# A two-layer transformer block on one core: opening work of ScalarE, VectorE, GpSimd and TensorE put in another order

## Chip, cores and metric

The kernel runs on 1 core of one Trainium2 chip. The metric is device microseconds (us) of one launch; lower is better. Engines are named as in the profile: PE (TensorE), DVE (VectorE), ACT (ScalarE), POOL (GpSimd), SP (the queue that issues DMAs). Each engine works through its own queue in order; semaphores tie the queues together.

## What is computed

Two adaLN layers are applied to x of shape 2 x 2048 x 128 (batch, tokens, features).

```python
mod = (silu(c) @ wmod)                      # six rows of 128 per batch: sa, ca, ga, sb, cb, gb
ga, gb = sign(ga) * max(|ga|, 0.25), sign(gb) * max(|gb|, 0.25)
h = layernorm(x) * (1 + ca) + sa
x = x + ga * attention(h)
h = layernorm(x) * (1 + cb) + sb
x = x + gb * ffn(h)
```

Layer 0's attention has q, k and v projections, rotary tables on q and k, and a mask that lets each token see itself, all before it and one after. Its feed-forward quantises inputs and weights in blocks of 16 to FP4 (scale = largest magnitude / 6, values rounded to the FP4 grid), and computes silu(gate) * up, then down. Layer 1's attention scores are h qk h^T, causal, and its feed-forward is a mixture of 8 experts with 2 chosen per token plus one shared expert.

## The kernel before

The work of a batch is written as 32 slots: slot s is one tile of 128 query tokens, slots 0 to 15 of layer 0's attention and 16 to 31 of layer 1's. Four tiles make a group of 512 tokens. Each engine has a loop over the slots, written out by hand, and other work (projections of the next group, layer norms, the feed-forward six and eight slots behind) is placed in it by slot numbers. In slot s PE computes the scores of tile s + 1 (`score_products`, L859 and L867), transposes the probabilities of tile s (L985) and multiplies them with the values (L1007); DVE takes the maximum of the new scores (`maximum`, L1836) and finishes the tile (`finish`, L1858 and L1859); ACT computes the exponentials (L1399) and copies the transposes (L1425).

**The opening** comes ahead of the slots. PE runs `WARM_UP` matmuls on ones (L818), transposes the conditioning vectors (L821), and, once the first modulation matrix has landed, multiplies it with silu(c) to get columns of scales (`columns`, L812). DVE turns them into gains, normalises the first group (`first_normalise`, L1600), PE transposes it (L788), ACT scales it (L1272), and PE projects keys and queries (`project_0`, L799). DVE rotates them (`open_rotate`, L1622 to L1626), ACT writes the rounded halves (`first_round`, L1299: fp32r high part), DVE the low parts (`open_low`, L1632). PE meanwhile computes layer 1's columns, the first values (L879), and `FIRST_WAIT` matmuls whose results nobody reads (`keep_clock`, L794); then come the first scores.

**Groups 1 to 3 of layer 0.** For each, DVE normalises (`normalise(2, ...)`, L1799, four tiles), PE transposes (L788), ACT scales (L1352), PE projects keys (in slots 0, 2, 4) and queries (slots 1, 3, 5) with L799, DVE multiplies with the tables (`rotate`, L1819), POOL sums (`rope_sum`, L710), ACT rounds (`round_rope`, L1453), and POOL takes the low part (`rope_low`, L716). POOL also computes 1/sqrt of the variance (`first_rsqrt`, L635) ahead of each normalisation and, from slot 4 on, the modulation of the feed-forward's input (`modulate_1`, L675 and L677).

**FP4 weights.** DVE scales them (L1649 to L1658) and builds the step of the grid (`fp4_grid`, L1663 and L1664, at the end of slot 0); POOL rounds them in three passes for each of gate, up and down (`round_fp4_weights`, L660, L662, L664; slots 1, 2 and 3, after `first_rsqrt`); PE transposes them (L804) and ACT copies them (`turned_fp4_weights`, L1306 to L1310), with a scaling of the down weights by the gains in slot 4 (L1497). In slot 4 DVE also prepares layer 1's gains (`layer1_gains`, L1573 to L1577 and L1673), ahead of its rotation of group 3's keys, and after the slot quantises the feed-forward's first input (`fp4_input`, from L1876 on).

```python
FP4_W_ROUND_SLOTS, FP4_W_TURN_SLOTS, FP4_W_GATE_SLOT = {1: 0, 2: 1, 3: 2}, {3: 2, 4: 3, 5: 4, 6: 5}, 4
WARM_UP, FIRST_WAIT = 12, 18
```

Of the kernel before, what the change touches and what calls it, by code (L numbers as in the profile page):

```python
# [24 lines left out]
BANK = 512  # L25
# [15 lines left out]
ACT = mybir.ActivationFunctionType  # L41
# [5 lines left out]
def score_chunks(layer, i):  # L47


    w = (i + 1) * P  # L50
    chunks = [(c, min(BANK, w - c)) for c in range(0, w, BANK)]
    if layer == 0 and i < TILES - 1:
        chunks[-1] = (chunks[-1][0], chunks[-1][1] + 1)
    return chunks
# [51 lines left out]
def early_group(slot, first):  # L106

    g, off = divmod(slot - first, 2)
    return g if off == 0 and 1 <= g < GROUPS else None
# [90 lines left out]

FP4_W_ROUND_SLOTS, FP4_W_TURN_SLOTS, FP4_W_GATE_SLOT = {1: 0, 2: 1, 3: 2}, {3: 2, 4: 3, 5: 4, 6: 5}, 4
FP4_W_BANKS, GAINS_SLOT = {2: 2, 3: 2, 4: 3, 5: 3}, 4
WARM_UP, FIRST_WAIT = 12, 18
NORM0_SLOT = K0_SLOT - 2
NORM1_SLOT, NORM2_SLOT, NORM3_SLOT = GROUP - 1, DOWN_LAG + GROUP - 1, TILES + GROUP - 1
FP4_SLOT = GROUP
# [51 lines left out]
def build(nc, x, cos, sin, wq, wk, wv, w_gate, w_up, w_down, c0, wmod0, qk, ov, gate_w, lb_bias,  # L260
          e_gate, e_up, e_down, s_gate, s_up, s_down, c1, wmod1, out):
    ctx = ExitStack()
    with ctx:
# [56 lines left out]
        tick = sb("tick", [P, 1])  # L320
# [81 lines left out]
        def bank(n, a=0, b=BANK, rows=P):  # L402
            return ps[0:rows, n * BANK + a:n * BANK + b]
# [3 lines left out]
        TURN, OUT_AT, GATE, UP = 4, 5, 6, 7  # L407
# [32 lines left out]
        first_high = sem("first_high")  # L440
# [10 lines left out]
        roped = sem("roped")  # L451
# [150 lines left out]
        def _(pool):  # L602
# [50 lines left out]
            def round_fp4_weights(k):  # L653

                name = "gud"[k]
                cols = slice(fp4_at[name], fp4_at[name] + (INNER if name == "d" else K_TILES * P))
                step = slice(cols.start // BLOCK, cols.stop // BLOCK)
                part = fp4_q[:, cols]
                pool.wait_ge(fp4_scaled, 1)
                pool.tensor_tensor(part, part, fp4_abs[:, cols], ALU.add).then_inc(fp4_rounded, 1)  # L660
                pool.wait_ge(fp4_rounded, 3 * k + 1)
                pool.tensor_tensor(part, part, fp4_abs[:, cols], ALU.subtract).then_inc(fp4_rounded, 1)  # L662
                pool.wait_ge(fp4_rounded, 3 * k + 2)
                pool.tensor_tensor(blocks(part), blocks(part), fp4_s[:, 1, step].unsqueeze(2).to_broadcast(  # L664
                    [P, step.stop - step.start, BLOCK]), ALU.mult).then_inc(fp4_rounded, 1)

            for b in range(BATCH):
# [64 lines left out]
                def rope_lows(s):  # L732
                    if early_group(s, K0_SLOT + 1) is not None:
                        rope_low(early_group(s, K0_SLOT + 1), 0)
                    if early_group(s, Q0_SLOT + 1) is not None:
                        rope_low(early_group(s, Q0_SLOT + 1), 1)
# [8 lines left out]
                for s in range(SLOTS):  # L745
                    at = lambda first: group_at(s, first)
                    if s < FP4_SLOT:
                        rope_lows(s)
                    if early_group(s, K0_SLOT) is not None:
                        rope_sum(early_group(s, K0_SLOT), 0)  # L750
                    if early_group(s, Q0_SLOT) is not None:
                        rope_sum(early_group(s, Q0_SLOT), 1)
                    if at(NORM1_SLOT + 1) is not None:
                        modulate_1(at(NORM1_SLOT + 1))
                    if at(Q1_SLOT) is not None:
                        q1_low(at(Q1_SLOT))
                    if ffn_tile(s, FFN_LAG) is not None:
                        hq_scaled(s - FFN_LAG)
                    if s >= FP4_SLOT:
                        rope_lows(s)  # L760
                    if b + 1 == BATCH and s == MOE_W_LOW_SLOT:
                        for k in range(-(-SPLIT_AT_ONCE // BANK)):
                            moe_w_low(k)
                    if early_group(s, NORM0_SLOT) is not None:
                        first_rsqrt(b * GROUPS + early_group(s, NORM0_SLOT) + 1)
                    if b == 0 and s in FP4_W_ROUND_SLOTS:
                        round_fp4_weights(FP4_W_ROUND_SLOTS[s])
                    if b + 1 < BATCH and s in (NEXT_SLOT - 2, NEXT_SLOT):
                        first_rsqrt((b + 1) * GROUPS + (s == NEXT_SLOT) + 1)
                    if s % GROUP == GROUP - 1:  # L770
                        scale_and_shift(1 + (at(NORM2_SLOT) is not None), b * 2 * GROUPS + s // GROUP + 1)
                    if at(NORM2_SLOT + 2) is not None:
                        keys_low(at(NORM2_SLOT + 2))
                    if at(FP4_SLOT) is not None:
                        xq_scaled(at(FP4_SLOT))
                    if b + 1 == BATCH:
                        if s == UNSEL_CLEAR_SLOT:
                            pool.wait_ge(v_proj_ready, BATCH * 2 * GROUPS)
                            pool.wait_ge(keys_ready, BATCH * GROUPS)
                            pool.memset(hT[:], 0.0).then_inc(unsel_zeroed, 1)  # L780
# [462 lines left out]

        @block.scalar
        def _(act):
            act.wait_ge(c_turned, 1)
            act.activation(silu_c[:], bank(TURN, 0, 2 * BATCH), ACT.Silu).then_inc(silu_ready, 1)
            act.wait_ge(zeroed, 10)
# [31 lines left out]
            rows = ps[:, 0:BATCH * BANK].rearrange("p (b n) -> p b n", b=BATCH)  # L1280
            act.activation(mod_row[:, :, 0, :], rows[:, :, 0:P], ACT.Copy)
            act.activation(mod_row[:, :, 1, :], rows[:, :, P:2 * P], ACT.Identity, bias=one).then_inc(rows_copied, 1)
            act.wait_ge(weights_turned, 2)
            act.activation(wv_g[:].rearrange("p b n -> p (b n)"), src[:, 0:BATCH * P], ACT.Copy).then_inc(weights_ready, 1)
            act.wait_ge(columns_ready, 3)
# [5 lines left out]
            ins.then_inc(mods_ready, 1)  # L1291
            act.wait_ge(rows_ready, 2)
            act.activation(ga1_row[:].rearrange("p b n -> p (b n)"), src[:, 0:BATCH * P], ACT.Copy).then_inc(rows_copied, 1)
            act.activation(tick[:], one, ACT.Exp)

            def first_round(which, src):

                act.wait_ge(roped, 2 * which + 2)
                act.activation((k_parts, q_parts)[which][0][:, 0:BANK], bank(src), ACT.Copy).then_inc(first_high, 1)  # L1299

            def turned_fp4_weights(n):

                act.wait_ge(weights_turned, n + 1)
# [21 lines left out]
                act.activation(probs[:, 0, start:start + width], ps[:, start:start + width], ACT.Exp,  # L1325
                               bias=neg_max[:, 0:1]).then_inc(exp_done, 1)

            first_round(0, UP)
            put_v_at(0, 0, GATE)
            first_round(1, 3)  # L1330
            first_exp(-1)
            for b in range(BATCH):
                def filled(key):
# [225 lines left out]
        def _(dve):  # L1559
# [227 lines left out]
            for b in range(BATCH):  # L1787
# [168 lines left out]

                for s in range(SLOTS):
                    following = len(score_chunks(*divmod(s + 1, TILES))) if s + 1 < SLOTS else 0
                    if following:
                        maximum(s + 1, 0)  # L1960
                    if b and s == 0:
# [29 lines left out]
                    if b + 1 == BATCH:  # L1991
                        route_in(s)
                    finish(s)
                    if b == 0 and s == 0:
                        fp4_grid()
                    if group_at(s, FP4_SLOT) is not None:
                        fp4_input(group_at(s, FP4_SLOT))
                    if group_at(s, LOGIT_SLOT) is not None:
# [98 lines left out]
```

## Time and profile before

| | us |
|---|---|
| runs, median of 3 | 669.61 (666.71 to 670.39) |
| profiled execution | 664.82 |
| its span in the trace | 663.0 |
| PE busy | 607.0 (92%) |
| DVE busy | 467.8 (71%) |
| ACT busy | 355.3 (54%) |
| POOL busy | 247.2 (37%) |

The span runs from the first to the last recorded instruction; 1.82 us of the profiled execution lie around it. Of the chain of work that ended last, 67% of the span is on PE, 15% on DVE, 9% on ACT, 4% on POOL. A busy PE is not one at its peak.

### The profile page before, as it was taken

The numbers are of one execution on the slowest core, as the hardware profiler recorded it, in microseconds if no ns is written. First come the engines' busy times: TensorE is split into PE (matmuls) and PEld (weight loads), VectorE is DVE, ScalarE is ACT, GpSimd is POOL, SyncE is SP. The second block draws the span as 40 slices with busy tenths as digits, with TensorE's granted clock in tenths as the row PEclk, the third lists the DMA queues.
The fourth block names the chain that finished last, engine by engine and source line by source line (L and its number), as shares of the span: only waits on it lengthen the run. The fifth ranks groups of instructions, "written<-read, shape, count | busy, mean of one in ns | idle before, by whom it ended". The sixth has DMA issues, their size and how long they took to land.

```text
span 663.0 us, 11002 instructions
## 1 busy us (share of the span) xinstructions
PE 607.0 (92%) x3758; PEld 478.1 (72%) x3780; DVE 467.8 (71%) x1265; ACT 355.3 (54%) x740; POOL 247.2 (37%) x305
## 2 busy tenths in 40 slices
PE   7977899988878899999989998978999999999997
PEld 5645677876666777886768787766677888777775
DVE  4867689786797456826658978679756674787765
ACT  3424454565545464554346456565566556666554
POOL 4256565454674322004465636457452100000000
PEclk9989999999999999999989999999999999999999
DMA  8300000000000000000000000020000000000111
GB/s 258 97 0 2 1 1 1 1 0 1 1 0 1 1 1 1 1 1 0 1 1 1 1 1 1 0 61 2 0 2 1 1 1 1 1 1 16 33 33 48
DMA packets 12494, 9.65 MB, mean 15 GB/s; under 512 B 1868, under 2 KB 10904, under 8 KB 12440
## 3 DMA queue, kind: packets, MB, share of 16 engines
q1 hardware_dynamic: 12440, 8.95, 4.5%
q8 instruction: 31, 0.51, 0.3%
q14 instruction: 23, 0.19, 0.1%
HBM read 6.84 MB, written 2.10 MB: 13 GB/s over the span
## 4 chain that ended last, share of the span: by engine, by line
PE 67%; DVE 15%; ACT 9%; POOL 4%; issue 4%; DVEq 0%; ACTq 0%; POOLq 0%
PE ps L1007 14%; PE ps L859 11%; PE ps L985 8%; PE ps L1191 5%; PE ps L799 4%; PE ps L1193 4%; PE ps L1192 4%; ACT xn L1359 2%; PE ps L1033 2%; PE ps L1034 2%; PE ps L1051 2%; PE ps L794 2%; POOL rstd L644 1%; PE ps L879 1%; DVE row_max L1836 1%
## 5 line engine op out<-in xcount | busy, mean ns | idle before, releaser
L1425 ACT ACTIVATE probsT<-ps 128x512 f32<-128x512 f32 (+3 forms) x160 | 85.4, 534 | 159.0 <-PE ps L985 159.0
L1007 PE MATMUL ps<-v_sb,probsT 128*128 128x129 f32 (+1 forms) x1124 | 152.0, 278 | 2.6 <-ACT probsT L1427 2.6
L1007 PEld LDWEIGHTS ps<-v_sb,probsT 128*128 128x128 f32 (+1 forms) x1124 | 137.8, 191 | 7.3 <-ACT probsT L1427 4.0
L1836 DVE TENSOR_REDUCE row_max<-ps 128x1 f32<-128x512 f32 (+2 forms) x144 | 87.4, 619 | 53.2 <-PE ps L867 26.7
L985 PE MATMUL ps<-ident,probs 128*128 128x128 f32 (+1 forms) x562 | 90.6, 277 | 16.1 <-ACT hT L1352 7.8
L985 PEld LDWEIGHTS ps<-ident,probs 128*128 128x128 f32 (+1 forms) x562 | 63.6, 139 | 48.0 <-issue 43.6
L1399 ACT ACTIVATE probs<-ps,neg_max 128x512 f32<-128x512 f32 (+7 forms) x158 | 93.1, 621 | 7.7 <-DVE neg_max L1843 7.0
L683 POOL TENSOR_TENSOR hq<-ha,hp 128x352 f32<-128x352 f32 x32 | 29.9, 935 | 100.9 <-DVE hp L1886 100.9
L859 PE MATMUL ps<-k_high,q_high 128*128 128x512 f32 (+5 forms) x100 | 42.5, 425 | 6.9 <-ACT probs L1399 6.9
L643 POOL TENSOR_SCALAR minus_mean<-mv 128x4 f32<-128x4 f32 (+1 forms) x16 | 3.8, 237 | 105.1 <-DVE veps L1586 104.9
L1858 DVE RECIPROCAL rsum<-ps 128x1 f32<-128x1 f32 x64 | 10.5, 164 | 41.6 <-PE ps L1007 41.2
L859 PE MATMUL ps<-h_high,q_high 128*128 128x512 f32 (+2 forms) x80 | 35.9, 449 | 3.1 <-POOL q_low L729 3.1
L1520 ACT ACTIVATE probs<-ps 128x512 f32<-128x512 f32 x40 | 24.0, 600 | 26.4 <-PE ps L1184 18.5
L859 PE MATMUL ps<-k_high,q_low 128*128 128x512 f32 (+5 forms) x100 | 34.6, 346 | 0.0
L859 PE MATMUL ps<-k_low,q_high 128*128 128x512 f32 (+5 forms) x100 | 34.5, 345 | 0.0
L1900 DVE SCALAR_TENSOR_TENSOR silu_g<-silu_g,ps 128x352 f32<-128x352 f32 x32 | 16.5, 515 | 23.7 <-ACT silu_g L1407 23.7
L1051 PE MATMUL ps<-w_dg,hqT 128*128 128x128 f32 (+1 forms) x192 | 28.0, 282 | 4.5 <-ACT hqT L1412 4.5
L685 POOL TENSOR_TENSOR hq<-hq,hp 128x352 f32<-128x352 f32 x32 | 29.9, 936 | 2.5
L1359 ACT ACTIVATE xn<-x_sb,shift,rstd 128x128 f32<-128x128 f32 x64 | 26.1, 482 | 8.3 <-POOL shift L646 8.3
L1793 DVE BATCH_NORM_STATS2 bn<-x_sb 128x6 f32<-128x128 f32 x112 | 28.4, 287 | 2.2
L1051 PEld LDWEIGHTS ps<-w_dg,hqT 128*128 128x128 f32 (+1 forms) x192 | 24.6, 191 | 7.0 <-ACT hqT L1412 6.3
L859 PE MATMUL ps<-h_high,q_low 128*128 128x512 f32 (+2 forms) x80 | 29.3, 366 | 0.0
(294 smaller groups left out, 1399.1 us busy)
## 6 DMA issues: line engine op xcount, KB each, us to landing
out<-x_sb SPq DMA_DIRECT2D x7, 256.0 KB, 2.3
hT_all<-in_L_wmod SPq DMA_DIRECT2D x2, 384.0 KB, 4.5
x_sb<-in_L_attn_x SPq DMA_DIRECT2D x2, 256.0 KB, 3.8
rope_cos<-table_cos SPq DMA_DIRECT2D x2, 256.0 KB, 4.5
rope_sin<-table_sin SPq DMA_DIRECT2D x2, 256.0 KB, 5.6
x_sb<-in_L_attn_x SPq DMA_DIRECT2D x1, 512.0 KB, 6.1
rope_cos<-table_cos SPq DMA_DIRECT2D x1, 512.0 KB, 7.1
rope_sin<-table_sin SPq DMA_DIRECT2D x1, 512.0 KB, 7.3
```

Source lines behind the costliest of these rows:

```text
L683: pool.tensor_tensor(hq[:, n % 2, :], ha[:], hp[:], ALU.add).then_inc(hq_step, 1)
L685: pool.tensor_tensor(hq[:, n % 2, :], hq[:, n % 2, :], hp[:], ALU.subtract).then_inc(hq_step, 1)
L859: mm = pe.matmul(ps[:, cols], q_parts[q][:, tile], keys[k][:, cols], start=(n == 0), stop=(stop and n == len(passes) - 1))
L985: mm = pe.transpose(bank(TURN, k * P, (k + 1) * P, size), probs[:, s % 2, j * P:j * P + size], ident[:])
L1007: mm = pe.matmul(bank(OUT_AT, 0, V_W), probsT[0:size, n % 4, k * P:(k + 1) * P], v_sb[0:size, j, :], start=(c == 0 and k == 0), stop=(c == ...
L1051: mm = pe.matmul(bank(OUT_AT, DOWN.start, DOWN.stop), hqT[0:size, k * P:(k + 1) * P], w_dg[0:size, bass.ds(b, 1), k, :].rearrange("p a n - ...
L1191: pe.matmul(dst, weights[0], high, start=start, stop=False)
L1359: return act.activation(xn[:, g, t * P:(t + 1) * P], x_sb[:, b * TILES + g * GROUP + t, :], ACT.Identity, scale=rstd[:, kind, t:t + 1], bi ...
L1399: act.activation(probs[:, s % 2, start:start + width], ps[:, start:start + width], ACT.Exp, bias=neg_max[:, s % 2:s % 2 + 1]).then_inc(exp ...
L1425: ins = act.activation(probsT[:, n % 4, 0:full], bank(TURN, 0, full), ACT.Copy)
L1793: return dve.bn_stats(bn[:, kind, t % GROUP, :], x_tile(t))
L1836: ins = dve.tensor_reduce(dst, ps[:, start:start + width], AX.X, ALU.max, negate=single)
```

## The change

- WARM_UP goes from 12 to 6, FIRST_WAIT from 18 to 13.
- On ACT the load of the exponential's table (with `tick`) and the rounding of the first keys move ahead of the copy of the scaled value weights, of layer 1's columns and of its gain row; the rounding of the first queries moves ahead of the first values.
- `fp4_grid` moves on DVE from the end of slot 0 to the head of slot 2.
- `round_fp4_weights` moves on POOL: gate and up to slot 2, ahead of `rope_sum` of group 2's keys; down to slot 4, ahead of `rope_sum` of group 3's keys.
- The scaling of the down weights moves from slot 4 to 5; their transposes and copies from slots 5 and 6 to 6 and 7.

No instruction is added other than by the move, six warm-up and five keep-clock matmuls go, and no DMA is moved.

```diff
-FP4_W_ROUND_SLOTS, FP4_W_TURN_SLOTS, FP4_W_GATE_SLOT = {1: 0, 2: 1, 3: 2}, {3: 2, 4: 3, 5: 4, 6: 5}, 4
+FP4_W_GRID_SLOT, FP4_W_ROUND_SLOTS = 2, {2: (0, 1), 4: (2,)}
+FP4_W_TURN_SLOTS, FP4_W_GATE_SLOT = {3: 2, 4: 3, 6: 4, 7: 5}, 5
-WARM_UP, FIRST_WAIT = 12, 18
+WARM_UP, FIRST_WAIT = 6, 13
...
                     if s < FP4_SLOT:
                         rope_lows(s)
+                    for k in FP4_W_ROUND_SLOTS.get(s, ()) if b == 0 else ():
+                        round_fp4_weights(k)
                     if early_group(s, K0_SLOT) is not None:
                         rope_sum(early_group(s, K0_SLOT), 0)
...
-                    if b == 0 and s in FP4_W_ROUND_SLOTS:
-                        round_fp4_weights(FP4_W_ROUND_SLOTS[s])
...
             act.activation(mod_row[:, :, 1, :], rows[:, :, P:2 * P], ACT.Identity, bias=one).then_inc(rows_copied, 1)
+            act.activation(tick[:], one, ACT.Exp)
+            first_round(0, UP)
             act.wait_ge(weights_turned, 2)
...
-            first_round(0, UP)
+            first_round(1, 3)
             put_v_at(0, 0, GATE)
-            first_round(1, 3)
             first_exp(-1)
...
                     following = len(score_chunks(*divmod(s + 1, TILES))) if s + 1 < SLOTS else 0
+                    if b == 0 and s == FP4_W_GRID_SLOT:
+                        fp4_grid()
                     if following:
                         maximum(s + 1, 0)
...
                     finish(s)
-                    if b == 0 and s == 0:
-                        fp4_grid()
```

In the changed kernel most lines stand one further down (L1836 to L1859 and L1573 to L1819 on DVE stand where they stood).

DVE, from the end of slot 0 on (L1793 is the last statistic of slot 0's tile), before:

```order
L1793 BN_STATS bn<-x_sb 128x6
L1663 TENSOR_SCALAR hT_all<-hT_all 128x1120
L1664 TENSOR_SCALAR hT_all<-hT_all 128x1120
L1836 TENSOR_REDUCE neg_max<-ps 128x1
L1819 TENSOR_TENSOR rope_t<-ps,rope_cos 128x512
L1819 TENSOR_TENSOR rope_t<-ps,rope_sin 128x512
L1799 TENSOR_SCALAR xn<-x_sb,mv,rstd 128x128 x4
```

and now:

```order
L1793 BN_STATS bn<-x_sb 128x6
L1836 TENSOR_REDUCE neg_max<-ps 128x1
L1819 TENSOR_TENSOR rope_t<-ps,rope_cos 128x512
L1819 TENSOR_TENSOR rope_t<-ps,rope_sin 128x512
L1799 TENSOR_SCALAR xn<-x_sb,mv,rstd 128x128 x4
L1858 RECIPROCAL rsum<-ps 128x1
L1859 SCALAR_TENSOR_TENSOR x_sb<-ps,rsum,x_sb 128x128
L1793 BN_STATS bn<-x_sb 128x6
L1663 TENSOR_SCALAR hT_all<-hT_all 128x1120
L1664 TENSOR_SCALAR hT_all<-hT_all 128x1120
L1836 TENSOR_REDUCE neg_max<-ps 128x1
```

The two operations of the grid have gone past the whole of slot 1.

POOL, slots 1 to 3 from the sum of group 1's queries on (L710 is `rope_sum`, L716 `rope_low`, L660 to L664 one of the weight matrices), before:

```order
L710 TENSOR_TENSOR rope_t<-rope_t 128x512
L660 TENSOR_TENSOR hT_all<-hT_all 128x384
L662 TENSOR_TENSOR hT_all<-hT_all 128x384
L664 TENSOR_TENSOR hT_all<-hT_all,fp_s 128x384
L716 TENSOR_TENSOR q_low<-rope_t,q_high 128x512
L710 TENSOR_TENSOR rope_t<-rope_t 128x512
L635 TENSOR_TENSOR rstd<-veps,half 128x4
L660 TENSOR_TENSOR hT_all<-hT_all 128x384
L662 TENSOR_TENSOR hT_all<-hT_all 128x384
L664 TENSOR_TENSOR hT_all<-hT_all,fp_s 128x384
L716 TENSOR_TENSOR k_low<-rope_t,k_high 128x512
L710 TENSOR_TENSOR rope_t<-rope_t 128x512
```

and now (one line further down):

```order
L711 TENSOR_TENSOR rope_t<-rope_t 128x512
L717 TENSOR_TENSOR q_low<-rope_t,q_high 128x512
L661 TENSOR_TENSOR hT_all<-hT_all 128x384
L663 TENSOR_TENSOR hT_all<-hT_all 128x384
L665 TENSOR_TENSOR hT_all<-hT_all,fp_s 128x384
L661 TENSOR_TENSOR hT_all<-hT_all 128x384
L663 TENSOR_TENSOR hT_all<-hT_all 128x384
L665 TENSOR_TENSOR hT_all<-hT_all,fp_s 128x384
L711 TENSOR_TENSOR rope_t<-rope_t 128x512
L636 TENSOR_TENSOR rstd<-veps,half 128x4
L717 TENSOR_TENSOR k_low<-rope_t,k_high 128x512
L711 TENSOR_TENSOR rope_t<-rope_t 128x512
```

Gate and up now stand together between the low part of group 1's queries and the sum of group 2's keys; down, which stood after the last row, has moved on into slot 4.

ACT, in the opening from the second half of the modulation row on, before:

```order
L1282 ACTIVATE mod_row<-ps,ones 128x2x128
L1284 ACTIVATE wv_g<-ps 128x256
L1288 ACTIVATE mod_col<-ps 128x2 x3
L1290 ACTIVATE mod_col<-ps,ones 128x2 x2
L1293 ACTIVATE ga_row<-ps 128x256
L1294 ACT_TABLE_LOAD
L1294 ACTIVATE tick<-ones 128x1
L1299 ACTIVATE k_high<-ps 128x512
L1318 ACTIVATE v_sb<-ps 128x4x128
L1299 ACTIVATE q_high<-ps 128x512
```

and now:

```order
L1288 ACTIVATE mod_row<-ps,ones 128x2x128
L1289 ACT_TABLE_LOAD
L1289 ACTIVATE tick<-ones 128x1
L1250 ACTIVATE k_high<-ps 128x512
L1292 ACTIVATE wv_g<-ps 128x256
L1296 ACTIVATE mod_col<-ps 128x2 x3
L1298 ACTIVATE mod_col<-ps,ones 128x2 x2
L1301 ACTIVATE ga_row<-ps 128x256
L1250 ACTIVATE q_high<-ps 128x512
L1319 ACTIVATE v_sb<-ps 128x4x128
```

The table load and the keys' high part have moved ahead of five copies, and the queries' high part ahead of the first values.

## Rows read from the trace of the kernel before

**Rows 1.** The page's slices: granted clock of PE, tenths of full speed, forty equal slices.

```profile
PEclk9989999999999999999989999999999999999999
```

**Rows 2.** Chain of work that ended last, opening: start us, us, what, instructions.

```profile
2.11 5.47 PE ps L818 x24
...
8.04 1.08 PE ps L812 x8
...
11.17 0.67 PE ps L788 x4
...
12.85 3.67 PE ps L799 x8
...
19.25 3.83 PE ps L794 x17
```

**Rows 3.** Timeline, opening: start us, us, engine, line, operation, out<-in, shapes, count [idle before].

```profile
1.88 0.51 SPq L535 DMA_DIRECT2D hT_all<-in_L_wmod  x1
...
18.74 1.28 ACT L1294 ACT_TABLE_LOAD   x1
...
21.73 0.69 DVE L1632 TENSOR_TENSOR q_low<-ps,q_high 128x512 fp32r<-128x512 f32 x1 [0.28 <-ACT q_high L1299]
```

**Rows 4.** DMA issues, the one at 1.88: KB, us from issue to landing.

```profile
hT_all<-in_L_wmod SPq DMA_DIRECT2D x1, 384.0 KB, 3.5
```

**Rows 5.** Chain of work that ended last, slots 0 to 3.

```profile
30.78 0.98 PE ps L799 x2
...
34.96 3.50 DVE xn L1799 x4
...
39.36 1.28 PE ps L859 x3
...
48.09 0.89 PE ps L859 x3
...
52.34 3.86 DVE xn L1799 x4
```

**Rows 6.** Timeline, slots 1 to 3.

```profile
31.22 1.48 POOL L716 TENSOR_TENSOR k_low<-rope_t,k_high 128x512 fp32r<-128x512 f32 x1
...
31.58 1.02 PE L799 MATMUL ps<-hT,wqrT 128*128 128x512 f32 x2
...
31.61 1.69 DVE L1664 TENSOR_SCALAR hT_all<-hT_all 128x1120 f32<-128x1120 f32 x1
...
35.04 1.30 POOL L710 TENSOR_TENSOR rope_t<-rope_t 128x512 f32<-128x512 f32 x1 [2.34 <-DVE rope_t L1819]
...
36.30 0.99 POOL L660 TENSOR_TENSOR hT_all<-hT_all 128x384 f32<-128x384 f32 x1
...
38.50 0.86 PE L788 MATMUL ps<-ident,xn 128*128 128x128 f32 x4 [3.07 <-DVE xn L1799]
...
40.77 1.26 POOL L716 TENSOR_TENSOR q_low<-rope_t,q_high 128x512 fp32r<-128x512 f32 x1 [1.48 <-ACT q_high L1453]
...
46.38 1.27 POOL L710 TENSOR_TENSOR rope_t<-rope_t 128x512 f32<-128x512 f32 x1 [4.35 <-DVE rope_t L1819]
```

**Rows 7.** Windows: stretch, length, busy of PE, PEld, DVE, ACT, POOL; clock, DMA share, GB/s.

```profile
39.00:40.00 1.00, 1.00 (x4) 0.82 (x3) 0.24 (x1) 0.61 (x1) 0.29 (x1) 0.50 0.00 0
...
42.00:43.00 1.00, 1.00 (x8) 0.86 (x8) 0.09 (x1) 0.12 (x1) 0.03 (x1) 0.88 0.00 0
```

**Rows 8.** Timeline, slots 4 to 6.

```profile
59.25 0.29 DVE L1573 TENSOR_SCALAR hT_all<-ga_row 128x256 f32<-128x256 f32 x1
...
61.63 0.69 DVE L1819 TENSOR_TENSOR rope_t<-ps,rope_cos 128x512 f32<-128x512 f32 x1
...
67.27 0.69 DVE L1876 TENSOR_REDUCE qs<-xn 128x32 f32<-128x512 f32 x1 [1.63 <-POOL xn L677]
...
72.84 0.16 DVE L1843 TENSOR_REDUCE neg_max<-row_max 128x1 f32<-128x2 f32 x1
...
73.93 1.15 ACT L1399 ACTIVATE probs<-ps,neg_max 128x512 f32<-128x512 f32 x2
```

More of the change, by code:

```diff
@@ L1245, in _, with first_round @@
         def _(act):
+            def first_round(which, src):
+                act.wait_ge(roped, 2 * which + 2)
+                act.activation((k_parts, q_parts)[which][0][:, 0:BANK], bank(src), ACT.Copy).then_inc(first_high, 1)
             act.wait_ge(c_turned, 1)
@@ L1293, in _ @@
             act.activation(ga1_row[:].rearrange("p b n -> p (b n)"), src[:, 0:BATCH * P], ACT.Copy).then_inc(rows_copied, 1)
[L1294 to L1299, printed above, removed]
             def turned_fp4_weights(n):
```

## The prediction

> **What bounds the kernel now.** I read the page's slices first, for the clock: PE runs at its full level nearly everywhere and falls twice, early in each batch [rows 1]. Then the chain of waits, which shows whom the others wait for in the first 75 us, all that this change can touch; then the timeline around each long piece of it, for what runs beside it.
>
> The opening is a chain through PE. Twelve warm-up matmuls (24 passes) hold it from 2.11 to 7.58; the columns follow at 8.04, the first transposes at 11.17, the projections at 12.85, the kept-clock matmuls from 19.25 to 23.08, then the scores [rows 2]. ACT and DVE get the last operand ready at 22.42, just ahead of PE [rows 3]. In slots 1 to 3 the chain twice sits in the four normalising operations on DVE, 3.50 and 3.86 us [rows 5]; before the transposes at 38.50 PE is idle for 3.07 us [rows 6], and behind that gap the granted clock is 0.50, the 1.2 GHz level, until a little past 42 [rows 7]. In slots 4 to 6 the chain goes through POOL, DVE and ACT by turns [rows 8].
>
> A piece saved here should last to the end, since all loads that these stages wait for are issued at times that the change doesn't touch, and none is late. The moved steps issue no DMA and pass none on SP.
>
> **The opening: 3.1 us.** The warm-up's passes take 5.47 / 24 = 0.23 us; a 128-column share of the projections takes 3.67 / 8 / 4 = 0.115 [rows 2]. So they run at 1.2 GHz, the projections at 2.4. Half of the passes end at 4.85. The columns then wait for silu(c), about 5.4, and the modulation matrix, landed at 1.88 + 3.5 = 5.38 [rows 3, 4]: 2.6 us earlier at best. From below: if the weights that are transposed next land only at 9.12, where PE took them, the gain is the idle ahead of 11.17, about 0.6 [rows 2]. If the clock is low until the projections, columns, row products and transposes cost 1.2 us more, which leaves 1.4. I take 2.0, between this and the best.
>
> Eighteen kept-clock matmuls take 3.83 us, 0.213 each; five fewer give 1.06 [rows 2]. The new order on ACT allows it: the table load of 1.28 us at 18.74 no longer stands between the rotation and the queries' rounding, so the last low part ends near 20.65 instead of 22.42 [rows 3], still ahead of PE's new 22.0. PE stays the one waited for, and the further 1.4 us that ACT saves is worth nothing. The five copies that the keys' rounding now precedes start 0.1 us later, with their consumers behind PE's columns anyway.
>
> The slots follow in the old times, as if the opening stood still.
>
> **The grid out of slot 0 (1.7 us).** The scores of slot 2 are ready at 30.78 [rows 5], but DVE is in the grid until 31.61 + 1.69 = 33.30, 0.6 us behind the end of POOL's low part (31.22 + 1.48 = 32.70): most of these 1.69 us are waiting for POOL [rows 6]. Without the grid, the maximum runs from 30.95, and the rotation is held by PE alone, whose second projection ends at 31.58 + 1.02 = 32.60 [rows 6]. With 0.7 us for the product DVE reaches the normalisation at 33.3 instead of 34.96.
>
> **The weight passes away from it (1.4 us more).** Before, each of its four operations ends with a POOL operation: first the sum (35.04 to 36.34), then weight passes of 0.99 us from 36.30 on [rows 6]. Now only the sum stands beside it. One operation is held until 33.4 + 1.3 = 34.7, the others take about 0.3, and the four end near 35.4 instead of 38.46: 3.05 us in all.
>
> **The clock (1.5 us more).** With PE not idle ahead of the transposes, the low level should not come. Three score passes of 512 columns take 0.89 there instead of 1.28 [rows 5]; over transposes, scores and values this makes about 1.5 us, so the keys' projection of slot 2 starts 4.5 us earlier.
>
> **Six weight passes ahead of the sum of slot 2 (3.1 us given back).** This is the wait that the change adds. The queries' low part now runs at about 37.6 to 38.9 instead of 40.77 to 42.03 [rows 6]. The grid, on DVE from 36.3 to 37.6, is done by then; it delays slot 3's maximum by 0.4 us, which nobody waits for. Six passes of about 1 us take POOL to 45.0, so the sum of group 2's keys starts 3.4 us after its products are there, and 1.4 before its old 46.38 [rows 6]. ACT's rounding stands behind it, and behind that the copy for which PE waits. Then 1/sqrt (about 1.0), a low part and a sum (1.3 each) run to 50.0. DVE starts the last normalisation at 47.45, is held by these two, and ends at 50.6 instead of 52.34 + 3.86 = 56.20 [rows 5]: **5.6 us earlier**, since the down weights have left this place.
>
> **The down weights beside layer 1's gains (2.8 us given back).** They now run from 53.65 to 56.5, while DVE prepares the gains, 52.85 to 56.3 at the old pace. Six of these operations are wide (0.29 to 0.42 us); before, no long POOL operation stood beside them [rows 8]. Nearest are the normalising operations, each of which lasted until POOL's ended [rows 5, 6]. If the gains' operations behave likewise, three passes hold three of them, 2.8 us less the overlap: 2.4. If only those of the same form (one tensor, scalars) do, two are held: 1.9. If none, 0. I take 2.4. Then the rotation starts at 58.8 instead of 61.63, 2.8 us earlier and not 5.6; sum, modulation and quantisation follow, the last at 64.5 instead of 67.27 [rows 8].
>
> The page SBUF — State Buffer of the Trainium skill, section Who interferes with whom, says that a DVE operation with two SBUF inputs is locked out by a GpSimd operation that reads SBUF, as one with a scalar in a two-port mode is, whichever starts second. By that the wide operations with two tensors are held too, and the loss is the 2.4; no row here shows that form alone.
>
> **Slots 4 to 7 (0.9 us won, 0.4 back).** ACT gives the scaling of the down weights to slot 5, where it used to wait for their transposes; I cost that at nothing. Slot 6's maximum is ready at 70.2 instead of 73.00, and the exponential, which ACT's queue held until 73.93, starts at 70.25 [rows 8]: **3.7 us**. Slot 7 gets one weight copy on ACT and three transposes on PE: 0.4 us back, between 0 and 1.0. The slots give **3.3 us**.
>
> **Sum.** 3.1 + 3.3 = 6.4 us. Against the profiled execution, 664.82, that is 658.4. This execution lies 4.8 under the median of the runs, 669.61, against which the forecast stands: 669.6 - 6.4 = **663.2 us**, by itself 661 to 665.5.
>
> **Rivals.** *The clock rises only during the projections.* The opening then gains 1.4 + 1.06 less 1.7 (two projections at half rate), 0.8, and the time is 665.5. For it: the whole warm-up runs low now, and 3.07 us of idleness were enough to lose the level [rows 2, 6, 7]. Against: PE is hardly idle between the shorter warm-up and the columns. The page TensorE: Matmul & The Clock Gate of the Trainium skill, section What's actually happening, has the throttled state as the default, which activity releases; that speaks against half a warm-up, and by that rule alone this rival would be the case.
>
> *The level stays low until the first scores: slower.* PE's unbroken work from 12.85 to 19.2 then takes 12.7 us instead of 6.35, thirteen kept-clock matmuls 5.5. Starting at 11.45, the scores come at 29.7 instead of 23.08, 6.6 later; less 3.3 this is 3.3 slower, 672.9, and with the kept-clock matmuls' successors low too, above 673. It decides from the moment at which the low level lasts past about 23 us, where work at half rate has eaten 5.8 us, all the rest. Against it: behind the gap at 38.50 the level was back after 3.7 us of dense work [rows 6, 7].
>
> *The gains are not held.* The rotation of slot 4 starts 5.2 us earlier, slot 6's exponential 6.1, and the time is 660.8. For it: their operations come in short pieces that may slip between POOL's.
>
> *The gain is lost again.* With DVE and POOL behind, PE idles some 2 us in slot 5. If its clock falls there as behind 38.50, 1.7 us go: 664.9; with a late clock in the opening as well, 667.2, no change that can be told.
>
> That the moves don't take place is excluded: the rows of the order show them.
>
> **How the numbers follow.** Half a per cent, 3.35 us, is about what a measurement of this kernel tells from no change. The forecast has 0.42, the late clock 0.20, the gains not held 0.20, the lost gain 0.12, the slower case 0.06. Below 666.3, faster: the first and third nearly wholly, half of the second, a fifth of the fourth, 0.73 together. Above 673, slower: the slower case and little else, 0.05. Between: 0.22. The range takes the bounds of the opening (0.6 to 2.6), of the gains (0 to 2.8) and the spread of the runs: 658 to 668.5.
>
> **What would show it.** Right: columns near 5.4; normalisations near 2.1 us in slot 1 and 3.1 in slot 3; clock 1.00 where it was 0.50; six weight passes in a row on POOL, with ACT's rounding waiting behind them; operations of the gains near 1 us beside the down weights. Wrong: columns still at 8, a clock of 0.50 beyond 10 us, a normalisation as long as before, or a new idle stretch of PE over 3 us in slots 3 to 7.

## The result, and the profile after

The changed kernel has a median of 660.12 us (657.72 to 661.23), the kernel before, run beside it, 668.16 (666.66 to 670.39): ratio 0.9872, 95% interval 0.9827 to 0.9917, faster by more than half a per cent. The forecast was 663.2, in a range of 658 to 668.5. The profiled execution has 660.58 us, with a span of 658.8; against that of before (664.82) this is 4.2 us less, and not 8.0. Both numbers need an explanation.

The page's slices show two falls of the granted clock, at other places than before [rows 1]:

```profile
PEclk9998999999899999999999999999999999999999
```

The opening, in the chain of waits of the changed kernel (start us, us, what, instructions):

```profile
2.10 2.91 PE ps L819 x12
...
5.47 1.87 PE ps L813 x8
...
8.07 2.00 PE ps L832 x4
...
11.95 5.70 PE ps L800 x8
...
20.33 2.81 PE ps L795 x13
```

The columns start 2.57 us earlier than in [rows 2], the projections 0.90. Then the eight projection passes take 5.70 us instead of 3.67, and the five kept-clock matmuls that are gone give 1.02. The first scores start at 22.78, before at 22.73: the opening gave nothing.

The slots, in the timeline of the changed kernel (start us, us, engine, line, operation, out<-in, shapes, count [idle before]):

```profile
33.30 2.06 DVE L1799 TENSOR_SCALAR xn<-x_sb,mv,rstd 128x128 f32<-128x128 f32 x4
...
38.71 0.99 POOL L661 TENSOR_TENSOR hT_all<-hT_all 128x384 f32<-128x384 f32 x1
...
43.81 0.84 POOL L665 TENSOR_TENSOR hT_all<-hT_all,fp_s 128x384 f32<-128x384 f32 x1
...
44.61 1.27 POOL L711 TENSOR_TENSOR rope_t<-rope_t 128x512 f32<-128x512 f32 x1
...
45.91 0.63 ACT L1453 ACTIVATE k_high<-rope_t 128x512 fp32r<-128x512 f32 x1 [3.32 <-POOL rope_t L711]
...
47.51 0.15 DVE L1843 TENSOR_REDUCE neg_max<-row_max 128x1 f32<-128x2 f32 x1
...
47.58 2.34 DVE L1799 TENSOR_SCALAR xn<-x_sb,mv,rstd 128x128 f32<-128x128 f32 x4
...
52.99 0.99 DVE L1573 TENSOR_SCALAR hT_all<-ga_row 128x256 f32<-128x256 f32 x1
...
53.91 0.93 POOL L663 TENSOR_TENSOR hT_all<-hT_all 128x352 f32<-128x352 f32 x1
...
54.01 0.98 DVE L1574 TENSOR_SCALAR hT_all<-ga_row 128x256 f32<-128x256 f32 x1
...
54.91 0.79 POOL L665 TENSOR_TENSOR hT_all<-hT_all,fp_s 128x352 f32<-128x352 f32 x1
...
55.02 0.96 DVE L1575 SCALAR_TENSOR_TENSOR hT_all<-ga_row,hT_all 128x256 f32<-128x256 f32 x1
...
56.02 0.43 DVE L1576 SCALAR_TENSOR_TENSOR hT_all<-ga_row,hT_all 128x256 f32<-128x256 f32 x1
...
57.28 0.68 DVE L1819 TENSOR_TENSOR rope_t<-ps,rope_cos 128x512 f32<-128x512 f32 x1
...
62.91 0.69 DVE L1876 TENSOR_REDUCE qs<-xn 128x32 f32<-128x512 f32 x1 [3.04 <-POOL xn L678]
...
68.46 0.15 DVE L1843 TENSOR_REDUCE neg_max<-row_max 128x1 f32<-128x2 f32 x1
...
68.65 1.16 ACT L1399 ACTIVATE probs<-ps,neg_max 128x512 f32<-128x512 f32 x2 [0.44 <-DVE neg_max L1843]
...
75.70 0.15 DVE L1843 TENSOR_REDUCE neg_max<-row_max 128x1 f32<-128x2 f32 x1
```

The normalisations take 2.06 and 2.34 us where they took 3.56 and 3.94 in the timeline of before (the chain counts 3.50 and 3.86 of them [rows 5]). The six weight passes stand in a row before the sum at 44.61, and ACT's rounding waits for it. Three operations of the gains are held to about 1 us beside the down weights. The quantisation is 4.36 earlier than before, slot 6's maximum 4.38 [rows 8].

For the experiments I cut the time at four marks that every trace has: the first score pass, and the starts of the maxima (L1843, or that line as the kernel's edit shifts it) of slots 4, 6 and 7. A slot's maximum is that of its tile's scores. The columns are the first mark, the three distances, and what is left of the profiled execution's time. "Low" names the stretches of 3 us with a granted clock below 0.9 that lie between 30 and 80 us.

| kernel | first scores | to slot 4 | to slot 6 | to slot 7 | rest | time | low |
|---|---|---|---|---|---|---|---|
| before | 22.73 | 29.45 | 20.66 | 8.12 | 583.86 | 664.82 | 39 to 42 |
| before, e5 | 22.33 | 30.40 | 21.46 | 9.01 | 584.34 | 667.54 | 36 to 45, 66 to 72 |
| changed | 22.78 | 24.73 | 20.95 | 7.24 | 584.88 | 660.58 | 60 to 66 |
| changed, e10 | 22.88 | 24.71 | 20.96 | 8.47 | 584.48 | 661.50 | 60 to 66, 69 to 75 |
| e1 slots only | 22.77 | 24.72 | 20.99 | 8.56 | 585.48 | 662.52 | 69 to 75 |
| e2 opening only | 22.90 | 30.06 | 23.07 | 9.00 | 583.52 | 668.55 | 36 to 45, 57 to 60, 69 to 75 |
| e3 WARM_UP 12 | 21.28 | 24.71 | 20.98 | 8.46 | 584.80 | 660.23 | 66 to 72 |
| e4 gains in slot 6 | 23.27 | 24.73 | 18.87 | 9.58 | 584.26 | 660.71 | 60 to 66 |
| e6 grid in slot 0 | 20.75 | 27.94 | 20.74 | 9.73 | 584.71 | 663.87 | 36 to 39, 69 to 78 |
| e9 the same, PE filled | 22.08 | 26.37 | 20.95 | 7.23 | 584.94 | 661.57 | none |
| e7 down in slot 3 | 23.50 | 24.73 | 20.07 | 7.23 | 584.72 | 660.25 | none |
| e8 WARM_UP 12, gains in 11 | 21.21 | 24.74 | 18.82 | 7.23 | 585.71 | 657.71 | none |
| e11 and FIRST_WAIT 8 | 19.51 | 24.80 | 18.81 | 7.23 | 585.88 | 656.23 | none |
| e12 and down in slot 3 | 19.98 | 24.78 | 19.84 | 7.23 | 585.66 | 657.49 | none |

The distances repeat to 0.1 us wherever order and clock are alike. The first mark shifts with the moment at which the clock rises at the start (last section) and with the landing of the modulation matrix (columns from 5.47 in the changed kernel, from 6.17 in e4).

The rest runs from 583.5 to 585.9, and a piece of the change lies in it. From slot 8's maximum to slot 9's the three executions with the old place of the down weights' copies (before, e5, e2) take 7.02 us, the eleven with the new one 8.12 to 8.14. The timeline of the kernel before:

```profile
88.55 0.16 DVE L1843 TENSOR_REDUCE neg_max<-row_max 128x1 f32<-128x3 f32 x1
...
89.24 1.23 ACT L1399 ACTIVATE probs<-ps,neg_max 128x512 f32<-128x512 f32 x2
...
95.57 0.16 DVE L1843 TENSOR_REDUCE neg_max<-row_max 128x1 f32<-128x3 f32 x1
```

and of the changed kernel:

```profile
83.28 0.16 DVE L1843 TENSOR_REDUCE neg_max<-row_max 128x1 f32<-128x3 f32 x1
...
85.02 0.38 ACT L1310 ACTIVATE w_dg<-ps 128x256 f32<-128x256 f32 x1 [0.95 <-PE ps L805]
...
85.46 1.26 ACT L1399 ACTIVATE probs<-ps,neg_max 128x512 f32<-128x512 f32 x2
...
91.40 0.16 DVE L1843 TENSOR_REDUCE neg_max<-row_max 128x1 f32<-128x3 f32 x1
```

The last copy of the down weights (`w_dg`) now waits for PE's transposes ahead of slot 8's exponential, which starts 2.18 us after its maximum instead of 0.69. So the copies' new slots cost 1.1 us there; no run moves them alone.

### The profile page after: what moved, and what is told of

Its sections match the earlier page's. It is cut to its first block, busy times and chain, and to the rows that moved or that the text cites. A ratio compares the mean times of both kernels' runs of the same rounds, so it can differ in the third digit from the quotient of the medians.

```text
span 658.8 us, 10990 instructions
## 1 busy us (share of the span) xinstructions
PE 609.0 (92%) x3763; PEld 477.3 (72%) x3763; DVE 464.8 (71%) x1265; ACT 355.0 (54%) x740; POOL 246.5 (37%) x305
## 4 chain that ended last, share of the span: by engine, by line
PE 68%; DVE 13%; ACT 9%; POOL 5%; issue 4%; DVEq 0%; ACTq 0%; POOLq 0%
PE ps L1008 14%; PE ps L860 11%; PE ps L986 8%; PE ps L1192 4%; PE ps L1194 4%; PE ps L1193 4%; PE ps L800 4%; ACT xn L1359 2%; PE ps L1034 2%; PE ps L1035 2%; PE ps L1052 2%; POOL rstd L645 2%; DVE row_max L1836 2%; PE ps L795 2%; ACT probs L1399 1%
## 5 line engine op out<-in xcount | busy, mean ns | idle before, releaser
L1836 DVE TENSOR_REDUCE row_max<-ps 128x1 f32<-128x512 f32 (+2 forms) x144 | 87.5, 619 | 54.1 <-PE ps L868 26.7
L1793 DVE BATCH_NORM_STATS2 bn<-x_sb 128x6 f32<-128x128 f32 x112 | 28.4, 287 | 2.2
```

Source lines behind the costliest of these rows:

```text
L1793: return dve.bn_stats(bn[:, kind, t % GROUP, :], x_tile(t))
L1836: ins = dve.tensor_reduce(dst, ps[:, start:start + width], AX.X, ALU.max, negate=single)
```

## Experiments

**e1, e2: the change in two halves.** e1 has the slots' part of the diff on the kernel before; e2 has the opening's part (ACT's order and the two constants):

```diff
-WARM_UP, FIRST_WAIT = 12, 18
+WARM_UP, FIRST_WAIT = 6, 13
...
+            act.activation(tick[:], one, ACT.Exp)
+            first_round(0, UP)
```

> The kernel before with the slots' part of the change alone: grid step at the head of slot 2, the weights' rounding in slots 2 and 4, turns in slots 3, 4, 6 and 7; warm-up 12, FIRST_WAIT 18 and ScalarE's old order stay. Theory (the slots bring the gain, the opening brings none): 662 to 664 us against about 668 for the kernel before, first scores at 23.1 as before, first scores of slot 7 at 78 less 8.6 = 69.4 or so (74.66 before), no stretch at clock 0.50 between 38 and 43. Rival (the opening brings half of the gain, as I had predicted): 665 us or more is left to the slots. Rival (the difference comes from the clock's falls, which vary from execution to execution): time as before within 2 us whatever the marks in slots 2 to 7 say.

> The kernel before with the opening's part alone: keys rounded ahead of the columns on ScalarE, warm-up 6, FIRST_WAIT 13; grid, rounding and turns as before. Theory (six passes less are paid back by projections at half rate, and FIRST_WAIT's five matmuls of 0.21 us are all that is left): first scores at 22.0 to 23.2 (23.08 before), time within 1 us of the kernel before, 667 to 668. My prediction's sum: first scores at 20.0 and 665 us. Rival (PE falls to the low level until the scores): first scores after 24, 670 us or more.

e1: 662.32 us, ratio 0.9914 (0.9885 to 0.9942); e2: 668.12, ratio 1.0003 (0.9984 to 1.0021). The first theory holds on both: the slots bring the gain, the opening by itself none. e2 has its first scores at 22.90. In e1 the first scores of slot 7 came at 69.41, as forecast; behind them the clock was low, and slot 7's maximum came only at 77.04, 8.56 after slot 6's and not 7.24.

**e3: the warm-up restored.**

```diff
-WARM_UP, FIRST_WAIT = 6, 13
+WARM_UP, FIRST_WAIT = 12, 13
```

> The changed kernel with WARM_UP 12 instead of 6, FIRST_WAIT stays 13. Theory (the halved warm-up's 2.6 us are lost again because the projections of the first group then run at 0.85 us a pass of 512 columns instead of 0.43): passes of the projections 0.43 to 0.5 us in the mean, first scores at 23.1 less or more 0.5, time 660 within 1 us of the changed kernel. My prediction's term (warm-up's passes lie on the path and cost 2.0 to 2.6): first scores 25 to 25.7, time 662 to 663. Rival (the low level costs more later than it saves): 658 or less.

660.30 us, ratio 0.9893 (0.9868 to 0.9917): the time of the changed kernel. The chain of waits of e3, opening:

```profile
2.10 5.16 PE ps L819 x24
...
12.47 3.67 PE ps L800 x8
...
18.87 2.75 PE ps L795 x12
```

The projections start 0.52 later than with half the warm-up and are done 1.51 earlier; the first scores come at 21.28 instead of 22.78. I had expected no change there; between these two executions the halved warm-up costs 1.5 us. The profiled times are nevertheless nearly the same, and the window of slot 6 shows where the 1.5 us were lost again (stretch, length, busy of PE, PEld, DVE, ACT, POOL; clock, DMA share, GB/s):

```profile
69.00:72.00 3.00, 3.00 (x14) 2.64 (x13) 0.69 (x1) 0.75 (x2) 2.62 (x3) 0.56 0.00 0
```

The clock fell between the maxima of slots 6 and 7, whose distance is 8.46 instead of 7.24. The changed kernel has this fall too in one of its two profiles (e10), so it is not shown that the fall is why the medians agree.

**e4: layer 1's gains moved two slots on.**

```diff
-FP4_W_BANKS, GAINS_SLOT = {2: 2, 3: 2, 4: 3, 5: 3}, 4
+FP4_W_BANKS, GAINS_SLOT = {2: 2, 3: 2, 4: 3, 5: 3}, 6
```

> The changed kernel with layer 1's gains in slot 6 instead of slot 4. Theory (gains of 4 to 6 us on VectorE, three of them held to 1 us beside the down weights' passes, end last for the rotation in slot 4 and bring TensorE's idle 1.6 us at 58.5 and the clock's fall behind it): rotation at 53 instead of 57.3, TensorE's idle time at 58 gone, first scores of slot 7 1.6 to 4 us earlier, and of that 1.2 to 2.6 lost again in slot 6 where gains of about 5 stand before a gap of 2.9 on VectorE: 657 to 659 us. Rival (TensorE is full enough there that the wait is only moved): 660 within 1 us. Rival (gains in slot 6 hold the gate's product and the quantisation behind it, and TensorE waits in slot 7 or 8): 661 to 663.

660.65 us, ratio 0.9886 (0.9858 to 0.9913): no gain. The theory's first half came true (2.08 us less up to slot 6), its balance did not: slot 6 paid 2.34 for the gains, of which 0.83 came back by slot 8's maximum (6.75 from slot 7's instead of 7.58).

**e5: the kernel before, unchanged, for a second profile.**

> The kernel before, unchanged, for a second profile: the execution that I worked from had 664.8 us, its timed runs have a median of 667 to 668. Theory (TensorE's clock falls at other places from execution to execution, and the profiled execution had a cheap pattern): 666 to 669 us, the same marks to the first scores (23.1), and 2 to 4 us more behind them wherever a slice shows a lower granted clock. Rival (the early stage repeats to 0.3 us, and the difference lies outside the span or late in the kernel): the first maximum of slot 7 at 81.0 within 0.5.

668.54 us in the median, ratio 1.0021 (0.9995 to 1.0047); the profiled execution has 667.54. Windows of e5:

```profile
36.00:39.00 3.00, 0.91 (x5) 0.91 (x5) 2.76 (x6) 0.00 (x0) 2.72 (x3) 0.74 0.00 0
39.00:42.00 3.00, 3.00 (x13) 2.38 (x13) 0.69 (x1) 1.30 (x2) 1.26 (x1) 0.50 0.00 0
42.00:45.00 3.00, 3.00 (x11) 1.87 (x10) 0.00 (x0) 0.60 (x1) 0.00 (x0) 0.62 0.00 0
...
66.00:69.00 3.00, 1.14 (x3) 0.96 (x4) 1.33 (x3) 2.17 (x5) 2.92 (x3) 0.86 0.00 0
69.00:72.00 3.00, 3.00 (x5) 1.15 (x4) 2.86 (x7) 0.00 (x0) 0.77 (x3) 0.57 0.00 0
```

The low level (1.2 GHz) lasts on into the window at 42, where [rows 7] has 0.88 in the microsecond from 42, and it comes a second time in slot 6. By slot 7 that is 2.64 us more than in the execution I worked from (60.87 from the first scores to slot 7, against 58.23); the two profiled times differ by 2.72. My execution had a cheaper pattern than this one.

**e6, e9: the grid back at the end of slot 0; and the same with PE kept busy.** In e9 seven more filler matmuls precede each of two waits of PE:

```diff
-                    if b == 0 and s == FP4_W_GRID_SLOT:
-                        fp4_grid()
...
+                    if b == 0 and s == 0:
+                        fp4_grid()
```

```diff
+                        if not b and key == ("fp4_first", 0):
+                            bank_free(key)
+                            keep_clock(TURN, 7)
...
-                    keep_clock(TURN, WAITED_FOR.get(key, 0))
+                    keep_clock(TURN, WAITED_FOR.get(key, 0) + (7 if not b and key == ("norm0", 2) else 0))
```

> The changed kernel with the grid step back at the end of slot 0, all else as changed. My prediction's term: 1.7 us, since the two grid passes of 0.73 and 1.69 us stand ahead of slot 2's maximum; the first normalisation starts at 35.0 instead of 33.3 and the rotations behind it are 1.2 to 1.7 later, 661 to 662 us. Rival (VectorE's 2 us of idle time at 38.2, and POOL, which ends the later waits, take it in): maxima of slots 4 to 6 within 0.3 us and 660 us. Rival (the transposes of group 2 late enough that TensorE falls idle for 2 us and its clock with it): 1.5 more, 662 to 664.

> The kernel with the grid at the end of slot 0 (e6), with TensorE given seven more filler matmuls of 0.21 us ahead of each of two waits: that for group 2's normalisation in slot 1 to 2 (idle 1.56 us in e6) and that for the first part of the quantised input in slot 6 (idle 1.54). Nothing else moves. Theory (the grid step in slot 0 costs little by its own length; what it costs is TensorE's idle time at 33.5 and the fall of the clock behind it, and the fall at 70 again): no granted clock under 0.9 between 34 and 44, the maximum of slot 7 at 75.5 or earlier instead of 79.16, 660 to 662 us. Rival (the late rotation itself is what costs, through POOL's sums and VectorE): the clock is kept, but the maximum of slot 7 stays at 78 to 79 and the time at 664 to 666. Rival (the fillers end late and hold the transposes): later than e6.

e6: 665.11 us, ratio 0.9963 (0.9941 to 0.9985), slower than my term and than its rivals allowed; e9: 660.43, ratio 0.9886 (0.9855 to 0.9917). Eleven of e6's twelve runs have 663.50 to 666.59 us and one 659.48; e9's six have 659.63 to 662.72. Windows of e6:

```profile
36.00:39.00 3.00, 3.00 (x15) 2.48 (x14) 0.69 (x1) 1.00 (x2) 1.92 (x2) 0.51 0.00 0
...
69.00:72.00 3.00, 1.71 (x5) 1.35 (x5) 1.27 (x5) 1.33 (x3) 2.84 (x4) 0.61 0.00 0
72.00:75.00 3.00, 3.00 (x14) 2.67 (x13) 0.69 (x1) 0.99 (x2) 2.09 (x2) 0.50 0.00 0
75.00:78.00 3.00, 3.00 (x13) 1.85 (x12) 0.52 (x2) 0.67 (x2) 0.00 (x0) 0.75 0.01 1
```

and the same places in e9:

```profile
36.00:39.00 3.00, 2.95 (x23) 2.32 (x22) 1.70 (x6) 1.30 (x2) 0.59 (x1) 1.00 0.00 0
...
69.00:72.00 3.00, 1.71 (x12) 1.54 (x12) 1.91 (x6) 1.33 (x3) 2.84 (x4) 1.00 0.00 0
72.00:75.00 3.00, 2.66 (x15) 1.71 (x13) 0.10 (x2) 1.55 (x3) 2.05 (x2) 1.00 0.01 1
```

The fillers do no work that anyone reads, and both falls are gone. From the first scores to slot 4 e9 is 1.57 us shorter than e6, and from slot 6 to 7 2.50. So a fall of the clock is the cause of these 4.1 us, and not its companion: only PE's fillers were added. These places are from one profile of each kernel; that the runs differ as well speaks against chance. e9's maximum of slot 7 came at 76.63 and not by 75.5, since its first scores were 1.33 later than e6's. What separates e9 from the changed kernel is when the normalisation starts: 12.16 us after the first scores in e6 and in e9, 10.52 in the changed kernel. That is the 1.64 us by which the distances to slot 4 differ (26.37 and 24.73).

**e7: the down weights in slot 3.**

```diff
-FP4_W_GRID_SLOT, FP4_W_ROUND_SLOTS = 2, {2: (0, 1), 4: (2,)}
+FP4_W_GRID_SLOT, FP4_W_ROUND_SLOTS = 2, {2: (0, 1), 3: (2,)}
```

> The changed kernel with the down weights' rounding at the head of slot 3 instead of slot 4. Theory (a pass of the down weights holds whatever VectorE passes without PSUM run beside it, by about 1 us each, and POOL's rope sums stand behind the three): the gains take 2.9 us instead of 4.4, but the sum of slot 3's rotation comes 2.7 us later; rotation of slot 5 at 56 to 57 (57.28 in the changed kernel), 659 to 661 us. Rival (the normalisation at 47.6 is held again, as before the change: 3.9 instead of 2.34): its transposes at 51.5 or later instead of 49.98, 661 to 663 us.

659.40 us, ratio 0.9879 (0.9855 to 0.9904): what was forecast. The timeline of e7:

```profile
48.31 3.34 DVE L1799 TENSOR_SCALAR xn<-x_sb,mv,rstd 128x128 f32<-128x128 f32 x4
...
54.71 0.29 DVE L1573 TENSOR_SCALAR hT_all<-ga_row 128x256 f32<-128x256 f32 x1
```

The normalisation is held by 1.0 more, not by the rival's 1.6, and the gains are not held: slots 4 to 6 take 20.07 instead of 20.95. By the medians the two places can't be told apart.

**e8: WARM_UP 12 and the gains in slot 11; e10: the changed kernel again; e11, e12: further on.** e8 has `WARM_UP, FIRST_WAIT = 12, 13` and `GAINS_SLOT` 11. e11 has e8's edit and

```diff
-WARM_UP, FIRST_WAIT = 12, 13
+WARM_UP, FIRST_WAIT = 12, 8
```

and e12 has e7's edit besides.

> The changed kernel with WARM_UP 12 and the gains in slot 11. Theory (both terms measured apart are real: 1.5 us at the first scores for the warm-up, 1.6 us at the quantisation for gains that stand elsewhere, and what was lost again in slot 6 was the gains' own place and one fall of the clock): maximum of slot 7 at 72.5 to 74 (75.70 in the changed kernel), 656.5 to 659 us. Rival (TensorE's idle time in slots 5 and 6 is ended by ScalarE's order, and a fall of the clock follows whatever is done): 75.4 for that maximum and 660 us.

> The changed kernel, unchanged, beside the next two. Theory (places of the clock's falls vary, the sum of them does so by 2 us): 658 to 662, median 660; one fall in slots 4 to 6 at about the same place, since TensorE's idle time in slot 5 is in the order of the work. Rival (the fall at 60.6 was chance): no clock under 0.9 before 100 us, and 658 or less.

> WARM_UP 12, gains in slot 11, and FIRST_WAIT 8 instead of 13: in e8 the queries' low part ended at 20.15 and the fillers ran to 21.2. Theory (five fillers of 0.213 us lie on the path): first scores 1.06 earlier and 656.2 us, 1.0 under e8's 657.2. Rival (what the opening gives is taken back by a fall of the clock or by POOL further on, as the rounding of slot 2 waits for VectorE): 657 to 658. Rival (TensorE falls idle before the first scores and to its low level): 659 or more.

> As the run before it, with the down weights' rounding in slot 3 as in e7. Theory (with the gains gone from slot 4 nothing on VectorE is held by the passes there, and in slot 3 they hold the normalisation by 1.0, as e7 showed with 3.34 instead of 2.34): 0.5 to 1 more than the run before, 657 us. Rival (POOL's queue in slot 4 ends last, and is 3 us shorter): 655 to 656.

e8: 657.23 us, ratio 0.9853 (0.9833 to 0.9873). e10: 660.13, ratio 0.9878 (0.9848 to 0.9907). e11: 656.27, ratio 0.9826 (0.9797 to 0.9855). e12: 657.66, ratio 0.9864 (0.9827 to 0.9901). e10 had the low stretch from 60 on, as the theory said, and one more in slot 6; but PE's idle time there, which the theory took for the reason, was followed by a fall in some executions only (last section). The timeline of e8:

```profile
52.64 0.69 DVE L1819 TENSOR_TENSOR rope_t<-ps,rope_cos 128x512 f32<-128x512 f32 x1 [2.15 <-PE ps L800]
...
59.20 0.69 DVE L1876 TENSOR_REDUCE qs<-xn 128x32 f32<-128x512 f32 x1 [1.40 <-POOL xn L678]
...
64.77 0.15 DVE L1843 TENSOR_REDUCE neg_max<-row_max 128x1 f32<-128x2 f32 x1
...
72.00 0.15 DVE L1843 TENSOR_REDUCE neg_max<-row_max 128x1 f32<-128x2 f32 x1
```

Slots 4 to 6 take 18.82 instead of 20.95: the gains cost 2.13 there, their own length included. In slot 11 they cost 0.51: the maxima of slots 11 to 14 lie 33.31 apart instead of 32.80. Slot 7's maximum, at 72.00, was even earlier than forecast. e11 is the fastest of all, 3.9 us under the changed kernel of the same comparison. Its first scores come 1.70 before those of e8 and not 1.06: in the chains the fillers take 1.67 instead of 2.75, and the warm-up 4.41 instead of 5.10, since the clock rose earlier in this execution. So the 1.0 us between the medians of e8 and e11, which are of two comparisons, fits the five fillers but doesn't show them alone. e12 costs 1.03 more in slots 4 to 6, as e7 said; two of its six runs, at 662.44 and 662.62, are slower than all others of e11 and e12, and no trace shows why.

## Why the prediction was right, and where it was wrong

**Faster, and in the range:** yes, with a sum of 6.4 us against 8.0 by the medians of that comparison. That the sum came this near is partly luck. In the two profiles the opening gave nothing of its 3.1; the slots gave 5.3 up to slot 7's maximum (52.92 from the first scores instead of 58.23) and took 1.1 back behind it, 4.2 instead of the 3.3 forecast. The rest of the 8.0 lies in the base: the profile of before is 3.3 under the median of its runs, that of the changed kernel 0.5 above.

**The opening, 3.1 us forecast, nothing measured.** *Fewer kept-clock matmuls, 1.06:* right, 1.02 in the chain, and PE stayed the one waited for: q_low was done at 21.48, and the first scores stood behind the fillers until 22.78. *Half the warm-up, 2.0:* the step that failed. I had the first rival, "the clock rises only during the projections", at a chance of 0.20, and that is what happened: the first two of four pairs of passes ran at half rate in six of the seven profiled executions with WARM_UP 6. In the seventh, e6, all ran at the full rate (3.67 us), with first scores at 20.75. So even a rise of the clock in time was worth only half a microsecond against the long warm-up (21.28 and 21.21 at the same FIRST_WAIT), not 2.0; the others came 0.8 to 2.3 later. The rival's price, 0.8 us of gain, was too friendly, since the projections started 0.9 earlier and not 1.4, and their half rate cost 2.03 and not 1.7. The page "TensorE: Matmul & The Clock Gate" of the Trainium skill, section "What's actually happening", spoke for this rival: it has the throttled state as the default, which activity releases. The trace agrees: in the changed kernel the first passes of 512 columns start 0.85 us and more apart, the last 0.43.

**Slots 1 to 3.** *Grid 1.7, passes away from the normalisation 1.4, clock 1.5:* sizes right. The normalisation starts at 33.30 (forecast 33.3) and ends at 35.36 (35.4), 1.50 shorter than before; a fall costs 1.57 (e6 less e9). By distances to slot 4 the grid is 1.64 (e9 less changed), the fall 1.57, and what is left between before and e6, the weight passes above all, 1.51: together the 4.72 between 29.45 and 24.73. *Six passes ahead of the sum:* right; sum at 44.61 (forecast 45.0), last normalisation from 47.58 to 49.92 (47.45 to 50.6).

**Slots 4 to 6.** *Gains held, 2.4 back:* right in kind, too large. Three operations of 0.29 to 0.42 us took 0.96 to 0.99, 1.9 us more together; e7 shows them unheld. The two-tensor operation at 55.02 is held too, and the next of its form, at 56.02, behind POOL's last pass, is not (0.96 and 0.43). That agrees with the page "SBUF — State Buffer" of the Trainium skill, section "Who interferes with whom", by which a DVE operation with two SBUF inputs contends with a GpSimd operation that reads SBUF. Since the gains also began earlier than forecast (51.98 against 52.85), the rotation came at 57.28 and not 58.8, and slot 6's maximum at 68.46 instead of the forecast 70.2. *Slot 6, 0.9 won:* right; the exponential starts 0.19 after the maximum instead of 1.09, and the distance to slot 7 fell from 8.12 to 7.24 (a fall of the clock made it 8.5 in e10 and e3). *Slot 7, 0.4 back, between 0 and 1.0:* too small; it is the 1.1 us between the maxima of slots 8 and 9.

**Clock.** The rival "the gain is lost again" placed a fall in slot 5 and priced it at 1.7 us. The fall came, at 60 to 64:

```profile
60.00:63.00 3.00, 2.93 (x6) 1.66 (x7) 0.09 (x1) 0.38 (x2) 2.84 (x5) 0.57 0.00 0
```

It cost nothing: slots 4 to 6 take 20.95 and 20.96 with it (e10), 20.98 and 20.99 without (e3, e1). The path there goes through POOL and DVE, as the quantisation at 62.91 shows, for which DVE waited 3.04 us for POOL. The fall that costs is one slot later, 1.2 to 2.5 us, and stood in no term.

**The base.** I counted terms from an execution 4.8 us under the median and took the offset to be common to both kernels. It was not: e5 lost 2.6 us of it by slot 7, in and right behind its falls of the clock, and no execution of the new order that leaves the grid in slot 2 has a fall between the first scores and 60 us. That is in part why the medians differ by more than my profiles do. e5's profile, 667.54, is itself 1.0 under its median, and what the slower runs lose stands in no trace.

**Still open.** e1 is 2.2 us slower by its median than the changed kernel, though the opening gives nothing by the first mark; the two are of different comparisons, and the intervals of their ratios overlap. In the profiles 1.3 of it is the fall in slot 6, which e10 had too, so I can't say that it belongs to e1's order. e3, of e1's comparison, is 2.0 us faster, and 1.5 of that stands at the first mark (21.28 against 22.77; 0.4 of this is an earlier rise of the clock, as the projections start at 12.47 and not 12.89): without the halved warm-up the opening's part does give something. That the medians of e3 and of the changed kernel agree all the same stays open. Falls at 174 to 180, 324 to 342 and 438 to 456 us come in some executions and not in others, and filling those waits was not tried.

## What to carry to other kernels

Cut the time at marks that every variant has: distances that repeat to 0.1 us show a term of 1 us where the total swings by 3. Before adding up terms, take a second profile of the kernel before, and ask of each fall of the clock who ends last there: where another engine does, it can cost nothing; where PE does, a wait of 1.5 us can cost more behind it than the wait itself, and fillers in the wait can give nearly as much as moving the work (e9 against the changed kernel: 660.43 and 660.13). A warm-up is shortened only if the passes behind it keep the full rate; the matmuls that bridge a known wait are the ones to cut, down to when the operand is there.

## What the runs showed of the hardware

The same idle time of PE is not always followed by a fall. Ahead of the scores that PE computes in slot 5, all eleven executions with the new order of the weight passes had PE idle for 1.58 to 1.63 us; a fall followed in three (the changed kernel, with 0.57 in the window from 60, e10 and e4), none in the other eight.

The clock's column is no witness for the opening. In the changed kernel it shows 1.00 there, with pairs of passes of 2.05 and 1.92 us. In e9, where the same pairs take 2.05 and 1.91, it shows the low level:

```profile
9.00:12.00 3.00, 1.73 (x5) 1.21 (x6) 0.47 (x3) 1.53 (x5) 0.00 (x0) 0.50 1.00 343
12.00:15.00 3.00, 3.00 (x5) 1.07 (x4) 1.85 (x10) 1.95 (x4) 1.70 (x2) 0.50 1.06 299
```

So at the start the rate is to be read from the length of a pass. The views print 1.00 wherever the trace has no record of the level, and in the changed kernel its first record, the full level, stands at 16.04 us, between a slow pass and the fast ones. By these records the last rise ahead of the first scores came at 5.2 to 8.2 us in the seven executions with WARM_UP 12, and at 15.2 to 17.1 in six of the seven with WARM_UP 6; in e6, whose projections all ran at the full rate, it came at 11.65, ahead of them.

The two executions of the kernel before share one fall, at 336 to 339; beside it one has 39 to 42, the other 36 to 45, 66 to 72 and 450.
